# Graph attention with a split score product: seven products from the third query pair on, and another maker of the third key form

## The reference

```python
lQ, lK, lV = m @ Wlq, h @ Wlk, h @ Wlv + blv
gQ, gK, gV = m @ Wgq, mean(h) @ Wgk, mean(h) @ Wgv + bgv
es, eV     = m @ Wes, m @ Wev + bev
s  = where(adj, lQ @ lK.T / 16, -1e9)
g  = gQ @ gK.T / 16
M  = max(max(s, axis=1), g, es)
le, ge, ee = exp(s - M), exp(g - M), exp(es - M)
d  = sum(le) + ge + ee
out = x + maximum(le/d @ lV + ge/d * gV + ee/d * eV, m)
```

## Time and profile before

| what | value |
|---|---|
| median of three runs | 737.04 us |
| the profiled execution, span from first to last instruction | 734.2 us |
| what lies around the span in that execution | not shown; the median is 2.8 us above the span |
| TensorE matmuls busy | 722.9 us, 98% |
| VectorE / ScalarE / POOL busy | 570.9 / 531.8 / 431.8 us |
| granted TensorE clock | full in all of 40 slices |

### The profile page before, as it was taken

The page is one execution under the profiler, slowest core; times in us unless marked ns, Lnnn a source line. Parts: engine busy times, 40 slices in busy tenths (PEclk is TensorE's granted clock), DMA queues, the critical chain, the costliest instruction groups (busy, mean ns, idle before and its releaser), DMA issues.

```text
span 734.2 us, 15026 instructions
## 1 busy us (share of the span) xinstructions
PE 722.9 (98%) x5248; PEld 511.6 (70%) x5248; DVE 570.9 (78%) x1352; ACT 531.8 (72%) x705; POOL 431.8 (59%) x298
## 2 busy tenths in 40 slices
PE   8899999999999999999999999999999999999998
PEld 7567566676766776776767777676776777676777
DVE  6887888868787797878887887887878887876644
ACT  5865876776777677777877687678767777677690
POOL 3769689645555564556445555555546555654493
PEclk9999999999999999999999999999999999999999
DMA  7694577869789897987877798889878798887697
GB/s 246 137 180 105 118 164 157 162 144 196 154 179 167 166 178 140 203 154 176 173 170 159 152 202 143 189 158 175 176 167 163 152 208 150 178 166 179 117 173 166
DMA packets 364716, 121.93 MB, mean 166 GB/s; under 512 B 324832, under 2 KB 364640, under 8 KB 364640
## 3 DMA queue, kind: packets, MB, share of 16 engines
q1 hardware_dynamic: 364096, 120.44, 81.4%
q10 hardware_dynamic: 544, 0.52, 0.2%
HBM read 36.57 MB, written 4.19 MB: 56 GB/s over the span
## 4 chain that ended last, share of the span: by engine, by line
PE 87%; POOL 4%; DMA 3%; issue 2%; DVE 2%; ACT 2%; SPq 1%; DVEq 0%; ACTq 0%; POOLq 0%
PE ps_u L1104 14%; PE ps_u L1106 14%; PE ps_u L1108 14%; PE ps_x L1002 7%; PE ps_x L1003 7%; PE ps_x L1001 7%; PE ps_q L928 4%; PE ps_v L1001 4%; PE ps_v L1003 4%; PE ps_v L1002 3%; PE ps_w L1001 2%; PE ps_w L1002 2%; PE ps_w L1003 2%; DMA s<-x 1%; DMA hT<-v_rows 1%
## 5 line engine op out<-in xcount | busy, mean ns | idle before, releaser
L610 POOL TENSOR_TENSOR p_base<-s,p_base 128x1024 f16<-128x1024 f32 x112 | 242.3, 2163 | 227.7 <-ACT p_base L813 222.9
L1104 PE MATMUL ps_u<-v_rows,pT_base 128*128 128x256 f16 x968 | 263.8, 273 | 0.6 <-DMA pT_base<-bias 0.6
L1106 PE MATMUL ps_u<-v_rows,pT_base 128*128 128x256 f16 x968 | 263.9, 273 | 0.0
L1108 PE MATMUL ps_u<-v_rows,pT_base 128*128 128x256 f16 x968 | 263.8, 273 | 0.0
L776 ACT ACTIVATE bias<-adj,big 128x1024 f32<-128x1024 uint8 x127 | 156.4, 1237 | 139.9 <-DVE bmax L1471 131.6
L789 ACT ACTIVATE s<-s,negm,invc 128x1024 f32<-128x1024 f32 x128 | 157.0, 1227 | 6.9 <-DVE negm L1527 6.9
L813 ACT ACTIVATE p_base<-s 128x1024 f16<-128x1024 f32 x122 | 129.0, 1057 | 6.2 <-DMA hW<-p_base 1.1
L1104 PEld LDWEIGHTS ps_u<-v_rows,pT_base 128*128 128x128 f16 x968 | 94.7, 98 | 53.1 <-issue 0.8
L1106 PEld LDWEIGHTS ps_u<-v_rows,pT_base 128*128 128x128 f16 x968 | 94.7, 98 | 52.2
L1471 DVE CUSTOM_DVE_ANT_0 s<-ps_x,bias 128x512 f32<-128x512 f32 x128 | 87.2, 686 | 47.2 <-PE ps_x L1003 43.6
L1108 PEld LDWEIGHTS ps_u<-v_rows,pT_base 128*128 128x128 f16 x968 | 94.7, 98 | 11.0
(11 more groups left out here) (241 smaller groups left out, 1271.8 us busy)
## 6 DMA issues: line engine op xcount, KB each, us to landing
adj<-adj SPq DMA_DIRECT2D x64, 256.0 KB, 3.1
pT_base<-p_base SPq DMA_TRANSPOSE x238, 3.2
s<-x SPq DMA_DIRECT2D x7, 512.0 KB, 4.8
f32q<-mx SPq DMA_DIRECT2D x14, 256.0 KB, 3.7
xm<-x SPq DMA_DIRECT2D x14, 256.0 KB, 3.0
xm<-mx SPq DMA_DIRECT2D x14, 256.0 KB, 3.5
out<-t_sb SPq DMA_DIRECT2D x14, 256.0 KB, 2.5
mxT_f<-mxT SPq DMA_DIRECT2D x4, 256.0 KB, 3.0
```

Of the source, the lines that this page charges most:

```text
L610: nc.gpsimd.tensor_tensor(p_rows(u)[:, 1], s32[:, p % NS, u % 2], p_rows(u)[:, 0], ALU.subtract).then_inc(s_plo, 1)
L1104: nc.tensor.matmul(acc, turn[:, 0, j], v_rows[:, kc, 0:D], start=opens, stop=False, skip_group_check=True)
L1106: nc.tensor.matmul(acc, turn[:, 0, j], v_rows[:, kc, D:2 * D], start=False, stop=False, skip_group_check=True)
L1108: done = nc.tensor.matmul(acc, turn[:, 1, j], v_rows[:, kc, 0:D], start=False, stop=end, skip_group_check=True)
```

## The change

`PC` goes from 12 to 8: the third pair (steps 8 to 11) has seven products. All key forms are thus due four steps earlier. The third form is now summed on VectorE from t2, which POOL has in f32 in tw[:, 1], less the plain form (t3 = t2 - k11, in its two halves), into a tile t3w that shares t_sb; ScalarE and VectorE then split it as before, from SBUF. The matmuls with the identities, and eye16, go. POOL's order of the key forms changes: t1, t2, t4 of group 1 and t1 of group 2 all in step 4, the rest in steps 6 to 9, and from group 1 on t2 waits until VectorE has read the last t2. VectorE keeps p_low for units of steps below LOW_AT - 5 = 3 (before 5), POOL has those from step 8 of its program on. `wev_low` and the other due work of steps 8 to 11 stand in the second branch of VectorE's step.

```diff
-    PC = 12
+    PC = 8
+    LOW_AT = 8
+    T3_SUM_AT = {4: 0, 5: 1, 7: 2, 9: 3}
+    T3_AT = {5: 0, 6: 1, 8: 2, 10: 3}
...
+        t3w = t_sb[:, :, :].rearrange("p t d -> p (t d)")
...
         def low_on_dve(u):
-            return u // 2 + LAG_E < PC - 2
+            return u // 2 + LAG_E < LOW_AT
...
             def transpose_mx(n):
                 elif n == QH + 2:
-                    sp.wait_ge(s_t3, NG)
+                    sp.wait_ge(s_t4, NG)
...
             def keys_t2(g):
+                if g:
+                    pool.wait_ge(s_t3part, g)
...
-                if p in (4, 6, 8):
-                    keys_t1(p // 2 - 1)
-                    keys_t2(p // 2 - 1)
-                if p in (5, 7, 9):
-                    keys_t4((p - 3) // 2)
+                if p == 4:
+                    keys_t1(1)
+                    keys_t2(1)
+                    keys_t4(1)
+                    keys_t1(2)
+                if p == 6:
+                    keys_t2(2)
+                    keys_t4(2)
+                if p == 7:
+                    keys_t1(3)
+                if p == 8:
+                    keys_t2(3)
+                if p == 9:
+                    keys_t4(3)
...
             def keys_t3_high(g):
                 act.wait_ge(s_t3sum, g + 1)
-                nc.scalar.activation(plain(g, 0, 1, 0), ps_q[:, g % 2]...
+                act.wait_ge(s_t1, g + 1)
+                act.wait_ge(s_p7, PC - NG + g + 1)
+                nc.scalar.activation(plain(g, 0, 1, 0), t3w...
...
-                if p in (PC - 2, PC):
-                    keys_t3_high(p - PC + 2)
-                    keys_t3_high(p - PC + 3)
+                if p in T3_AT:
+                    keys_t3_high(T3_AT[p])
...
-                            if p == PC - 2 and t:
-                                keys_t3_sum(b)
...
-                    if p == PC:
-                        keys_t3_sum(2)
-                        keys_t3_sum(3)
...
+            def keys_t3_sum(g):
+                t3 = t3w.rearrange("p (j q) -> p j q", q=P)
+                dve.wait_ge(s_t2, g + 1)
+                if g:
+                    dve.wait_ge(s_t3, g)
+                nc.vector.tensor_tensor(t3, tw[:, 1]..., plain(g, 0, 0, 0), ALU.subtract).then_inc(s_t3part, 1)
+                dve.wait_ge(s_t3part, g + 1)
+                nc.vector.tensor_tensor(t3, t3, plain(g, 0, 0, 1), ALU.subtract).then_inc(s_t3sum, 1)
...
                     out22(p)
-                    if p == PC - 2:
-                        keys_t3_low(0)
-                        keys_t3_low(1)
+                    if p in T3_AT:
+                        keys_t3_low(T3_AT[p])
...
+                    if p in T3_SUM_AT:
+                        keys_t3_sum(T3_SUM_AT[p])
                     if p == 5:
                         weight_tops()
```

More of the change, by code:

```diff
@@ L186, in build @@
         cqs = sb("cqs", [P, 2])
-        eye16 = sb("eye16", [P, 2, P], F16)
         s_x = [sem(f"s_x{i}") for i in range(XG)]
@@ L219, in build @@
         s_t1, s_t2, s_t4, s_t3, s_tw = (sem(n) for n in ("s_t1", "s_t2", "s_t4", "s_t3", "s_tw"))
-        s_t3sum, s_t3hi, s_eye = (sem(n) for n in ("s_t3sum", "s_t3hi", "s_eye"))
+        s_t3part, s_t3sum, s_t3hi = (sem(n) for n in ("s_t3part", "s_t3sum", "s_t3hi"))
         s_bias = sem("s_bias")
@@ L816, in keys_t3_high @@
                 act.wait_ge(s_t3sum, g + 1)
-                nc.scalar.activation(plain(g, 0, 1, 0), ps_q[:, g % 2].rearrange("p (j q) -> p j q", q=P), ACT.Copy
+                act.wait_ge(s_t1, g + 1)
+                act.wait_ge(s_p7, PC - NG + g + 1)
+                nc.scalar.activation(plain(g, 0, 1, 0), t3w.rearrange("p (j q) -> p j q", q=P), ACT.Copy
                                      ).then_inc(s_t3hi, 1)
@@ L869, in _ @@
                         v_high(n)
-            act.wait_ge(s_const, 4)
-            for k in range(2):
-                nc.scalar.activation(eye16[:, k], ident, ACT.Copy, scale=1.0 - 2.0 * k).then_inc(s_eye, 1)
             mask_bias(7)
@@ L950, in project @@
                     pe.wait_ge(s_c2, 2 * (n - 3))
-                if n == PC // NG + 1:
-                    pe.wait_ge(s_t3, NG)
                 if n >= QH:
@@ L1111, in p_times_v @@
                         done.then_inc(s_pv, 1)
[L1113 to L1122, removed]
             def es_values(n):
-                if n == 0:
-                    pe.wait_ge(s_t3, 2)
                 if n < QH:
@@ L1230, in _ @@
                     v_product(n)
-            pe.wait_ge(s_eye, 2)
             pe.wait_ge(s_gev, 3)
@@ L1583, in local_rows @@
                                                    r12[:, t], ALU.mult, ALU.add).then_inc(s_c1, 1)
+            def keys_t3_sum(g):
[3 more added lines that the diff above has]
+                    dve.wait_ge(s_t3, g)
+                nc.vector.tensor_tensor(t3, tw[:, 1].rearrange("p (j q) -> p j q", q=P), plain(g, 0, 0, 0), ALU.subtract
+                                        ).then_inc(s_t3part, 1)
+                dve.wait_ge(s_t3part, g + 1)
+                nc.vector.tensor_tensor(t3, t3, plain(g, 0, 0, 1), ALU.subtract).then_inc(s_t3sum, 1)
             def keys_t3_low(g):
                 dve.wait_ge(s_t3hi, g + 1)
-                nc.vector.tensor_tensor(plain(g, 0, 1, 1), ps_q[:, g % 2].rearrange("p (j q) -> p j q", q=P),
+                nc.vector.tensor_tensor(plain(g, 0, 1, 1), t3w.rearrange("p (j q) -> p j q", q=P),
                                         plain(g, 0, 1, 0), ALU.subtract).then_inc(s_t3, 1)
@@ L1775, in _ @@
                         weights_low()
[L1776 to L1785, removed]
                 else:
@@ L1806, in _ @@
                         add12(p)
-                    if p == PC:
-                        keys_t3_low(2)
-                        keys_t3_low(3)
+                    if p in T3_AT:
+                        keys_t3_low(T3_AT[p])
                     if wino(old):
@@ L1826, in _ @@
                         row_max(n)
+                    if p in T3_SUM_AT:
+                        keys_t3_sum(T3_SUM_AT[p])
+                    if p == 9:
+                        wev_low()
                     if step == 1 and ended:
```

2 lines of the change are left out of this document (removed).

## The result

The changed kernel takes 756.5 us, the median of four runs (754.5 to 757.2). The kernel before took 737.5 beside it. The ratio is 1.024, with a 95% interval of 1.022 to 1.027. The forecast was 747.6 with a range of 740 to 754: the sign was right, the size wrong, and the range did not hold the time. The profiled execution has a span of 755.3 us and a time of 757.0, so 1.7 us lie around the span. Before, the span was 734.2; span against span, the change costs 21.1 us.

What follows compares the result with a forecast made beforehand. TensorE's work plus its few waits bounds the kernel. Matmuls removed give -6.1 us, the wait for out22(7) at step 8 +16.7, sum +10.6; span 734.2 + 10.6 + 2.8 around it = 747.6 us, range 740 to 754.

Steps and rivals of the forecast that it cites:

- Step 1: POOL's t2(1) waits for VectorE's first sum of t3(0), so it starts at 78.4 us, where it started at 72.79.
- Steps 2 to 4: POOL's forms (14.6 us), hold-ups (4.0) and q_sums (2.3) delay ScalarE's exp(3) to 100.2 us, 12.2 late.
- Step 5: VectorE's stretch from p_low(3) keeps its 14.4 us, plus 1.0 for keys_t3_low(1), so out22(7) ends at 118.05.
- the paragraph of the edits costed at nothing: Steps 8 to 11: VectorE's new adds, three of 0.69 us per step, are covered by removed p_lows and the late start.
- The fallback: If the cover for VectorE's adds in steps 8 to 11 is gone, some 2 us per step show.
- a gain of 6.1 us: TensorE loses four products in steps 8 to 11 (2.6 us) and the third form's 16 matmuls (3.5 us).
- Point 3: VectorE and POOL hold each other up: two p_lows and four t3 sums cost 4.0 us, so t1(2) ends at 97.0.
- Rival one: TensorE's clock falls to 1.2 GHz during the wait before step 8: +2.6 us, 750.2 us; chance 0.25.
- the case in which the clock stays full: The forecast itself: out22(7) late before step 8, clock full, +10.6 us, 747.6 us; chance 0.55.
- rival three: POOL falls behind for good, so its p_low(8) is late for TensorE in step 10: say 3 us, 750.6; chance 0.10.
- the upper bound: Every VectorE instruction held up by POOL adds its whole length before step 8: +13.7 us, 750.7 us.

Runs made afterwards that it cites:

- x1_order: Changed kernel with keys_t4(1) and keys_t1(2) moved on POOL from step 4 to step 6, behind the query sums: 751.4 us.
- x5_due: Kernel of x1_order with the sum of t3(3) moved to VectorE's step 10, its halves to step 11 and wev_low to step 13: 752.3 us.
- x2_no_t3: Changed kernel without VectorE's twelve instructions for the third key form (sums and low halves), semaphores still set: 745.8 us in one run.
- x3_busy: Changed kernel with 16 unread 512-column matmuls ahead of p1(8)'s wait, to keep TensorE busy: 754.8 us.
- x7_plow_first: Kernel of x5_due with t1 of group 3 moved on POOL from step 7 to 8, behind the low halves of units 6 and 7: 751.0 us.
- x8_order_no_t3: Changed kernel with the edits of x1_order and x2_no_t3 together: 747.6 us.
- x4_pe_sum: Kernel before with PC = 8, the third key form still summed on TensorE, and POOL's order kept but for keys_t1(3) in step 7: 747.1 us.
- x6_sum12: Kernel before (PC = 12, its POOL order) with the third key form summed on VectorE into PSUM instead of by identity matmuls: 742.3 us.

## Why the prediction was right in half, and where it failed

**Right: everything up to the opening of step 8.** Step 1: t2(1) was forecast for 78.4 and started at 79.28, after 5.64 us of idle time, and VectorE's L1582 ended that. Steps 2 to 4: POOL's sums began at 97.3 (97.0), q_high at 99.17 (99.3), exp(3) at 100.03 (100.2). Step 5: out22(7) ended at 116.78 + 0.69 = 117.5 (118.05). These agree within 0.9 us, but 1.0 us of late opening is in them, so the step 8 that was forecast 16.7 us late is 15.2 late through the change. The mechanism of the forecast is shown by x1_order: with two forms moved, q_high is 11.7 us earlier and p1(8) 8.2, of each 0.9 by an earlier opening.

**Failed: the paragraph of the edits costed at nothing.** It said that the work new on VectorE in steps 8 to 11 is covered, because these steps "start late with VectorE caught up". VectorE was not caught up: it was what made them late, and it went on almost without a pause, 40.0 of 42.7 us busy from 102.5 to 145.2. The fallback, some 2 us a step, was written down and then left out of the sum; one such wait, 4.1 us in step 10, came. x5_due shows that the sum of t3(3) and wev_low made it, on top of x1_order: with both moved it falls from 3.8 to 0.75. Between p1(8) and p1(13), where the forecast had a gain of 6.1 us and nothing against it, 8.1 us were lost.

**Failed: the new work behind step 8.** Point 3 gave four 512-wide sums 0.5 us extra each, and keys_t3_low(1) 1.0 in all. For those this was about right: the four took 4.6 us together, where 0.7 and 0.5 each make 4.8, and keys_t3_low(1) took 0.95. But from 117.39 on stand six more (the sums and low halves of t3(2) and t3(3)), 8.2 us in all, which the forecast left out. Measured, the twelve instructions took 1.26 us each, 15.2 together in place of 2.6, so 12.6 us were added to VectorE in steps 4 to 10. x2_no_t3 gives the price of all twelve: 10 us, 7.5 of them by p1(13).

**Rival one, the clock: it came, but not its price.** It had 0.25 and 2.6 us for one stretch. It happened in three stretches, not one; behind the first TensorE still waits 7.0 us for p1(8), and in the other two TensorE works about 2.1 and 1.5 us longer. x3_busy shows that taking the second away gives nothing by p1(13), since the waits behind it grow by as much. For the third there is no run. The Trainium skill (TensorE: Matmul & The Clock Gate, What's actually happening) has it that activity keeps the clock up and an idle array falls to half. The rows after agree: 0.50 behind waits of 7.03 and 3.96 us, and already behind 1.31 and 1.62 us with two tiny matmuls between them. I had the rule, and a forecast wait of 7.8 us, and still gave the case in which the clock stays full the greater chance.

**Too small: rival three, POOL.** It had 0.10 and was placed in step 10. In the changed kernel no long wait is put down to it. Where step 8 opens earlier, POOL is the next to hold the step: x1_order, x5_due, x7_plow_first and x8_order_no_t3 show it with 3.3, 3.0, 3.2 and 3.3 us, and x4_pe_sum, with another order on POOL, with 2.9 in step 11. x2_no_t3, which relieves VectorE and leaves POOL's order alone, does not show it. The rivals were priced as if each stood alone. Here they stand in one line, and a cured wait is in large part handed to the next.

**Against the forecast in numbers.** It had +10.6; the profile has +21.1. The 10.5 between them: 4.1 for step 10, 3.6 for TensorE's work at half clock (2.1 of which would have been waits at full clock), 3.1 - 0.4 for later waits, 1.0 for the opening, less 1.5 by which step 8's own lateness was overstated, which leaves 0.6 unexplained. (Against the median the miss is 8.9, since less lies around this profile's span, 1.7, than the 2.8 that I carried over.) The cause of the later waits (200, 219, 243, 294 to 330 us) stays open: x1_order has 0.8 us of them, x5_due 2.7, and no run was made for them. The range failed because its upper end held one bound of one case with a part of the clock's price, and no further wait. In the sums, the upper bound is 3 us above the middle, so +13.6 and not +13.7, which changes nothing.

## What to carry to other kernels

An engine that makes a step late has not caught up when the step begins: carry its backlog through the following steps, and put every new instruction there at full price. When two helpers feed the same engine with little room to spare, as VectorE and POOL do here (9.95 of 10.4 us each), a wait that is cured on the one can reappear on the other, so ask for each rival what stands behind it and not only whether it comes. Work taken from the engine that bounds the kernel is no gain where the engine that takes it has no room: here VectorE got 12.6 us for 3.5. And before a shorter time is put down to an edit, look where in the span it is shorter: x3_busy's 2.8 us lay where the edit had nothing to do.

## What the runs showed of the hardware

**Where an operand lies sets whether POOL can stop VectorE.** The low half of t3 takes 682 ns with one operand in PSUM and 1291 with both in SBUF, at the same size. In x4_pe_sum, which makes it from PSUM beside POOL's work, all four took 0.68 to 0.69. Two operands in SBUF are not slow by themselves: the first sum of the changed kernel ran with POOL idle and took 0.69, where the other three took up to 1.69.

```profile
78.51 0.69 DVE L1582 TENSOR_TENSOR t_sb<-tw,hT 128x512 f32<-128x512 f32 x1
```

The outs, which read PSUM and SBUF, took 0.69 us beside POOL in every row above. Tiny ones are stopped too: invc, a 128x2 instruction, took 1.09 us (138.71) beside POOL, and 0.15 at 17.80, as one instruction of POOL ended. And a result in PSUM does not help: L1577 of x6_sum12, with two f16 operands in SBUF, took 2.39 us. The Trainium skill (SBUF — State Buffer, SBUF: two separate sides) says that an instruction with two SBUF inputs or in a two-port mode takes the shared pair of ports for its whole length, the former only against a POOL instruction that reads SBUF. The rows agree for the instructions with two inputs; invc reads one tensor, and no row shows whether it ran in a two-port mode. The sharper half of that rule, two SBUF inputs or not, is what the forecast didn't use.

**Two short idle times close together were enough to halve the clock.** Around 1.31 and 1.62 us of idle time [93.31 and 95.31 above] the granted clock was 0.50 from 94.4 to 101.2. In the kernel before, one of 1.49 us by itself left it full.

**The opening varies by itself.** One transfer near 49 us ended a wait of 0.6 us in some executions and of 2.76 in others, and in x4_pe_sum this with its half clock made the opening 5.7 us longer. Two medians that differ by less than this are to be compared from a common point on.
